# A Mamba block's output product on TensorE with plain and gamma-scaled weights, in place of GpSimd's gamma multiplication, in a new order of work

## The reference, cut to what matters

```python
h = tokens(x)                                             # 64 x 197 x 192
xz = layernorm(h) @ W_in;  x_inner, z = split(xz)         # 384 + 384
x_conv = silu(conv4(x_inner) + conv_b)
B, C = split(x_conv @ W_x);  delta = softplus(x_conv @ W_dt + b_dt)
s_t = exp(delta_t * A) * s_(t-1) + delta_t * x_t * B_t    # 384 x 16 states, 197 steps
y = (sum over states of s_t * C_t + D * x_conv) * silu(z)
out = y @ W_out
h = h + (out - mean) / sqrt(var + 1e-5) * gamma + beta    # the norm of this change
out = h + moe(layernorm(h))
```

## Time and profile before

| | |
|---|---|
| three runs | 2906.84, 2912.44 (median), 2925.01 us |
| the profiled execution | 2912.24 us, its span 2910.5 us |
| PE, DVE, ACT, POOL busy | 2502.9, 2273.4, 2123.5, 2312.8 us |
| mean granted PE clock | 0.927 of 2.4 GHz |

### The profile page before, as it was taken

The page is one execution under the profiler, slowest core; times in us unless marked ns, Lnnn a source line. Parts: engine busy times, 40 slices in busy tenths (PEclk is TensorE's granted clock), DMA queues, the critical chain, the costliest instruction groups (busy, mean ns, idle before and its releaser), DMA issues. The chain is left out here.

```text
span 2910.5 us, 37983 instructions
## 1 busy us (share of the span) xinstructions
PE 2502.9 (86%) x12595; PEld 1554.2 (53%) x12595; DVE 2273.4 (78%) x2290; ACT 2123.5 (73%) x4560; POOL 2312.8 (79%) x1158
## 2 busy tenths in 40 slices
PE   7788888888888889888888888888875478999997
PEld 4444444444445444444444444554431367888886
DVE  2799999999999999999999999999999664222222
ACT  3688888888888888988888888888885343334332
POOL 0589999999999999999999999999998242544442
PEclk9898999999999998999999999999985689999999
DMA  3555544555544455555445554445541034666652
GB/s 102 130 117 117 116 109 109 119 128 118 118 109 109 109 124 117 124 125 115 109 110 130 126 117 109 109 109 133 127 108 33 26 124 148 221 204 219 204 193 87
DMA packets 165466, 361.09 MB, mean 124 GB/s; under 512 B 18353, under 2 KB 89593, under 8 KB 157848
## 3 DMA queue, kind: packets, MB, share of 16 engines
q1 hardware_dynamic: 152504, 329.59, 45.0%
q0 software_dynamic: 12768, 29.08, 3.1%
HBM read 293.86 MB, written 69.30 MB: 125 GB/s over the span
## 5 line engine op out<-in xcount | busy, mean ns | idle before, releaser
L1532 DVE TENSOR_TENSOR_SCAN arena<-banks,arena 128x788 f32<-128x788 f32 x768 | 1350.2, 1788 | 120.9 <-ACT banks L731 91.0
L531 POOL TENSOR_TENSOR arena<-arena 128x1576 f32<-128x1576 f32 x384 | 1246.9, 3259 | 23.6 <-DVE arena L1532 23.5
L731 ACT ACTIVATE banks<-arena,neg_a 128x392 f32<-128x392 f32 x1536 | 833.5, 580 | 60.8 <-DVE arena L1532 58.4
L1521 DVE TENSOR_TENSOR arena<-arena,banks 128x1576 f32<-128x1576 f32 x320 | 568.1, 1775 | 19.8 <-PE banks L1099 16.7
L1115 PE MATMUL banks<-arena,gather_q 128*32 128x394 f32 x3072 | 373.9, 562 | 12.3 <-POOL arena L531 11.7
L1065 PE MATMUL banks<-arena,v_lo 128*128 128x394 f32 x768 | 307.2, 546 | 35.9 <-ACT arena L803 19.5
L689 POOL DMA_INDIRECT out_tokens<-arena x114 | 114.7, 1006 | 265.8 <-DVE arena L1731 246.6
L1044 PE MATMUL banks<-wtok,arena 128*99 128x192 f32 x1536 | 266.5, 331 | 57.7 <-ACT arena L881 31.1
L1716 DVE TENSOR_TENSOR arena<-banks,arena 128x384 f32<-128x384 f32 x57 | 31.8, 558 | 360.9 <-PE banks L1402 316.1
L1044 PEld LDWEIGHTS banks<-wtok,arena 128*99 128x99 f32 x1536 | 246.3, 167 | 101.2 <-ACT arena L881 51.0
L1012 ACT ACTIVATE arena<-banks 128x256 f32<-128x256 f32 x57 | 22.0, 385 | 326.3 <-PE banks L1368 305.3
(11 more groups left out here) (247 smaller groups left out, 4391.4 us busy)
## 6 DMA issues: line engine op xcount, KB each, us to landing
arena<-delta_du_scratch SPq DMA_DIRECT2D x384, 394.0 KB, 10.6
arena<-in_w_pack SPq DMA_DIRECT2D x57, 1155.0 KB
delta_du_scratch<-arena SPq DMA_DIRECT2D x96, 394.0 KB, 3.2
arena<-in_x SPq DMA_DIRECT2D x32, 1176.0 KB, 12.1
rows_scratch<-arena SPq DMA_DIRECT2D x32, 297.0 KB
rows_scratch<-arena SPq DMA_DIRECT2D x32, 294.0 KB
arena<-in_b SPq DMA_DIRECT2D x57, 96.0 KB
arena<-in_conv_w SPq DMA_DIRECT2D x1, 2304.0 KB, 11.3
```

What stands on the lines that cost most here:

```text
L531: pool.tensor_tensor(v[:, :, :], v[:, :, :], c_rep[r][:, u % NG].unsqueeze(1).to_broadcast([P, NQ, N2]), ALU.mult).then_inc(s_mulp, 1)
L731: ins = act.activation(o, d, ACT.Exp, scale=neg_a[:, c:c + 1])
L1521: dve.tensor_tensor(hb[(UNITS * n + u) % BUFS][:, :, :], rep[m][:, :, 1, :], ps_b[:, 0:N2].unsqueeze(1).to_broadcast([P, NQ, N2]), ALU.mul ...
L1532: dve.tensor_tensor_scan(v, decay[k % 2], v, 0.0, ALU.mult, ALU.add).then_inc(s_scan, 1)
```

## The change

1. A second weight set `wgam` = centred `wout` times gamma is made once at the start (gamma is now spread over 128 partitions). New PE products `out_gamma` b = 0, 1 multiply y by it into banks of their own.
2. `copy_out` is gone. `out_squares` reads the plain product from PSUM; the new `copy_gamma` copies the scaled one to `ob`; `out_norm` scales that. `apply_gamma` is gone, and `add_residual` waits for `out_norm`.
3. The three small deviation steps leave ACT: POOL does each before its power, with one `tensor_scalar`, or two `tensor_tensor` for the rows. For out and front this puts two instructions in POOL's order where there was one before the power's own wait.
4. A new order on PE, ACT, DVE and POOL. `silu_z` moves next to `silu_x` with one `exp_ln_tables` for both. `row_stats`, `rstd_rows` and `row_norm` move from body i+2 to body i+1 of their pair. SP's order is unchanged; its store of a pair's rows waits for `row_norm` as before.

The functions:

```diff
-        gam = sb("gam", [H0, DIM])
+        gam = sb("gam", [P, DIM])
+            def out_gamma(n, o, b):
+                if b == 0:
+                    pe.wait_ge(s_yev, MB * (n + 1))
+                    pe.wait_ge(s_wc, 2)
+                v = kbank(OG[b], o)
+                for f in range(2):
+                    c = b * L + f * HSTEP
+                    for k in range(MB):
+                        mm = pe.matmul(v[0:H0, f * DIM:(f + 1) * DIM], y[:, k, c:c + H0], wgam[:, k, :], start=(k == 0),
+                                       stop=(k == MB - 1))
+                mm.then_inc(s_ogmm, 1)
...
+            def out_squares(n, r, o, b):
                 act.wait_ge(s_opmm, 2 * n + b + 1)
...
+                for f in range(2):
+                    c = 2 * b + f
+                    ins = act.activation(rows[r][:, c, DIM:2 * DIM], kbank(OUT[b], o)[0:H0, f * DIM:(f + 1) * DIM], ACT.Square,
+                                         accum_out=sq2[:, c:c + 1])
+                ins.then_inc(s_oev, 1)
...
             def rstd_out(n):
                 need(pool, s_onorm, n)
+                pool.wait_ge(s_oev, 2 * (n + 1))
+                pool.tensor_scalar(var2[:, :], sq2[:, :], 1.0 / DIM, EPS, ALU.mult, ALU.add).then_inc(s_var2, 1)
                 pool.wait_ge(s_var2, n + 1)
...
+            dve.tensor_tensor(wgam[:, :, :], wout[:, :, :], gam[:, :].unsqueeze(1).to_broadcast([P, MB, DIM]), ALU.mult).then_inc(s_wc, 1)
```

PE's order, cut to the places of which the prediction speaks:

```diff
+                    if 1 in on and u == 0:
+                        pe.wait_ge(s_gev, 10 * (i + 1) + 2)
+                        dt(i + 1, o, r, DT + 2)
+                    if 1 in on and u == 0:
+                        pe.wait_ge(s_gev, 10 * (i + 1) + 3)
+                        dt(i + 1, o, r, DT + 1)
+                    if 1 in on and u == 0:
+                        pe.wait_ge(s_gev, 10 * (i + 1) + 4)
+                        dt(i + 1, o, r, DT)
...
+                    if -1 in on and u == 5:
+                        if 2 in on:
+                            pe.wait_ge(s_h, 2 * (i + 2) + 2)
...
+                        out_product(i - 1, r, 0)
...
+                    if -2 in on and u == 5:
+                        if i == PAIRS + 1:
+                            rank(FIRST, 1)
...
-            rank(FIRST, 1)
```

More of the change, by code:

```diff
@@ L514, in rstd_front @@
                 need(pool, s_hn, n)
+                pool.wait_ge(s_sq1, n + 1)
+                pool.tensor_scalar(var1[:, :], sq1[:, :], 1.0 / DIM, EPS, ALU.mult, ALU.add).then_inc(s_var[0], 1)
                 pool.wait_ge(s_var[0], n + 1)
@@ L521, in rstd_rows @@
                 need(pool, s_rows, n)
+                pool.wait_ge(s_mv3, n + 1)
+                pool.tensor_tensor(mv3[:, :, 0], mv3[:, :, 0], small[0:H0, 1, :], ALU.mult)
+                pool.tensor_tensor(mv3[:, :, 1], mv3[:, :, 1], small[0:H0, 2, :], ALU.add).then_inc(s_var[2], 1)
                 pool.wait_ge(s_var[2], n + 1)
@@ L554, in fill_rows, with add_residual @@
                                    ALU.add).then_inc(s_hbeta, 1)
-            def apply_gamma(n):
+            def add_residual(n, r):
                 pool.wait_ge(s_onorm, n + 1)
[L558 to L562, removed]
                 pool.wait_ge(s_hbeta, n + 1)
@@ L648, in body @@
                     if -1 in on and u == 9:
-                        rstd_out(i - 1)
+                        add_residual(i - 1, o)
+                    if -1 in on and u == 10:
+                        rstd_rows(i - 1)
                     if 0 in on and u > 0:
@@ L900, in body @@
-                    if -2 in on and k == 3:
-                        row_norm(i - 2, r)
+                        copy_product(i + 1, o, o, 1)
+                    if 1 in on and k == 1:
+                        silu_x(i + 1, o)
+                        exp_ln_tables()
+                    if 1 in on and k == 2:
+                        copy_product(i + 1, o, r, DT + 2)
                     if 0 in on and k == 3:
                         keep_b(i)
+                    if 1 in on and k == 3:
+                        copy_product(i + 1, o, r, DT + 1)
@@ new lines, in body @@
+                    if 1 in on and k == 5:
+                        softplus_up(i + 1)
+                    if 1 in on and k == 6:
+                        softplus_t(i + 1)
+                    if 1 in on and k == 7:
+                        softplus_ln(i + 1)
+                    if 1 in on and k == 8:
+                        middle_bc(i + 1, o)
+                    if 0 in on and k == 10:
+                        copy_c(i, r, r, 3)
+                    if 2 in on and k == 11:
+                        front_squares(i + 2, r)
@@ new lines, in body @@
+                    if 1 in on and k == 13:
+                        third_bc(i + 1, o)
+                    if 1 in on and k == 14:
+                        copy_product(i + 1, o, r, Z + 1)
+                    if -1 in on and k == 15:
+                        out_squares(i - 1, o, r, 1)
+                    if -1 in on and k == 16:
+                        copy_gamma(i - 1, r, 1)
+                    if -2 in on and k == 17:
+                        copy_back_t(i - 2, r, 1)
+                    if 2 in on and k == 17:
+                        front_norm(i + 2, r)
@@ L1612, in body @@
                         scan(i, k)
[L1613 to L1617 removed]
+                    if -1 in on and k == 5:
                         if i == PAIRS:
```

378 lines of the change are left out of this document (161 added, 217 removed).

## The result

The changed kernel takes 2927.68 us (2916.30 to 2935.11, 20 runs), the kernel before, in the same comparison, 2910.59 (2891.11 to 2928.18, 20 runs). The ratio is 1.0047, with a 95% interval of 1.0030 to 1.0064: slower by half a per cent, where I had forecast 0.6% faster. The profiled execution took 2930.19, its span is 2928.5, 18.0 more than that of before.

The account below looks back on a forecast made before the run. DVE and POOL, within 3 us of the period and joined by waits over ACT and PE, bound it. 64.5 + 1.8 + 0.1 + 0.7 = 67.1 us a pair against 67.45 (-10.5), ends -7.8: 2894 us, range 2862 to 2946.

Parts of the forecast that it names:

- within 1%: Whole kernel: a time that can't be told from no change, between 2883 and 2942 us; chance 0.42.
- DVE does the same work in another order: 64.5 a pair without waits.: DVE among the pairs: own work unchanged by the new order, 64.5 us a pair, to which new waits are added.
- a tensor_scalar of 4 columns isn't in the trace: POOL's new deviation step: no such instruction to price it by, between 0.20 and 1.02 us, taken as 0.20.
- Step A: Start of a pair: dt products wait for silu_x and delay spread_b(2) and bx(2); 1.5 to 2.2 us lost, taken as 1.8.
- my slow-dt rival: dt products at half rate behind PE's 2.1 us wait for silu_x: 68.7 us a pair, 2942 us; chance 0.27.
- Step B: From take_y0 to scan 18: PE waits under 1 us, scan 18 loses nothing, bx_pool9 0.1 us.
- step D: Back of a pair, behind decays 18: out_norm, add_residual, row_stats and row_norm all in time by tenths; cost 0.
- Step C: At out_product0: PE waits 3.0 us for embed1, the clock falls, decays 12 and 13 come late; 0.7 us lost.
- POOL, 64.5.: POOL's own need a pair: falls by 0.8 to 64.5 us without apply_gamma, tying with DVE's 64.5.
- The start, -2.: First pair: bc no longer ahead of dt on PE, 6 matmuls or 2 us before the first delta; -2 us.
- The end, -5.8.: Behind the last pair: DVE's 5.77 us wait for the first rank products goes as they move earlier; -5.8 us.

Follow-up runs that it names:

- The second form tried here: The changed kernel with front_stats' negated mean on DVE as a scalar_tensor_tensor with two SBUF inputs instead of a tensor_scalar; ratio 1.0024 to the kernel before.
- the kernel whose GpSimd was busy for 98.9% of the window: The kernel before, in its old order with gamma on POOL, with only front_stats' negated mean moved from DVE to ACT; 2849.54 us, ratio 0.9757.

## Why the prediction was wrong

The forecast was 2894, 0.6% faster; it is 0.5% slower. The measured time lies in the range of 2862 to 2946 and, by the 1% that I had named, in "within 1%"; the sign was wrong.

*"DVE does the same work in another order: 64.5 a pair without waits."* This is the step that failed. It was 65.07. It took every duration of before as the instruction's own. That of front_stats was set by where a POOL instruction happened to end, 0.55 to 1.07 us among the pairs, and the change moved that place, to 1.22 to 1.85. This is +0.70 a pair in the mean, 20 us, of a term that I had put at no change without a reason. I had also written that a tensor_scalar of 4 columns isn't in the trace. POOL had none, but front_stats on DVE is one, and its 0.56 beside the 0.20 that I took would have been the hint.

The Trainium skill (SBUF — State Buffer, SBUF: two separate sides) says that VectorE and GpSimd share a pair of ports, and that whichever starts first holds it for its whole instruction. The trace agrees in the main: 60 of 60 end with a POOL instruction. The section counts a VectorE operation in a two-port mode and, against a GpSimd operation that reads SBUF, one with two inputs in SBUF as users of the pair. The second form tried here has two such inputs, and it waits; whether the tensor_scalar ran in a two-port mode no run here shows. In two other runs one VectorE instruction of 30 was held not by the one POOL instruction that had started before it, but by three more that started behind it. The section would have warned of this step; I hadn't weighed it.

*Step A, 1.8 us (1.5 to 2.2).* It cost 0.82 + 1.33 + 0.28 = 2.43, which is +0.63 and nearly as much as the step above. The size was off because my forecast and my slow-dt rival are both true, in different pairs: dt takes 7.9 us in 19 of 30 and 6.2 in the others. The rival had 3.4 for the step (1.5 + 1.9); its pairs show 0.83 + 1.90 + 0.29 = 3.0. I had given it 0.27, and 19 of 30 pairs took its way.

*Step B, 0.1.* Right. PE waited 0.51 for take_y0 in the pair shown and 0.90 in the mean, kept its clock in all 29, and scan 18 has no gap. But the wait in front of scan 20, which was to go with it, stayed (0.29 before and 0.32 now in the mean); I count it under step D.

*Step C, 0.7.* Too high: 0.37 in the mean. out_product0 waited 1.20 for embed1, not 3.0, and ran at full rate (2.19 for 12). The clock fell later, behind a further 1.41, at z (the first two of L1075 took 1.68 in place of 0.82), and cost 1.08 at scan 14 in the ten of 29 periods in which dt had been fast.

*Step D, 0.* Nearly right: 0.32 at scan 20; the row norms themselves are in time, and the residual waits for out_norm 0.3 us at most.

*POOL, 64.5.* Right, if anything too high: the tensor_scalar took 0.20 to 0.21 as taken. But that it "ties" with DVE didn't hold once DVE's own need was 65.07: POOL idled 3.1 us a pair for scans. The offload was worth nothing in the time (the new order with gamma on POOL: 1.0040 against 1.0047), because the 1 us that it spares DVE at row_stats went into slow dt products.

*The start, -2.* It was +3.8. I had seen dt come earlier and not what bc then delays. The first bx, before, then after:

```profile
92.18 1.80 DVE L1521 TENSOR_TENSOR arena<-arena,banks 128x1576 f32<-128x1576 f32 x1 [16.75 <-PE banks L1099]
```

```profile
95.64 1.80 DVE L1530 TENSOR_TENSOR arena<-arena,banks 128x1576 f32<-128x1576 f32 x1 [17.82 <-PE banks L1084]
```

It waits for spread_b(0), which on PE stands behind the tokens' products. These now stand behind bc and start at 68.10 in place of 66.11. spread_b(0) itself now also stands behind a second conv product.

*The end, -5.8.* It was -8.4, and the 5.77 of the earlier trace rows are gone as said.

In sums: 67.1 became 67.1 + 0.57 (DVE's own time) + 0.63 (A) - 0.1 (B) - 0.33 (C) + 0.32 (D) = 68.2, as measured. That step C was too large by 0.33, and hides a part of the 1.2 us by which the first two terms were too small, is luck.

What stays open: why the same wait of 1.97 us leaves dt at full clock in some pairs and not in others. With gamma on POOL in the new order, 3 of 30 pairs were slow, behind waits of the same length. And why step D left 0.32 at scan 20 was not tried.

## What to carry to other kernels

A small instruction whose duration in the profile varies, here from 0.17 to 1.85 us, can hide a wait inside its busy time: compare its end with the ends on the other engines before you take its price, and treat that price as one that any new order can change. Relieving an engine pays only when it is what the others wait for, and a ratio of 1 can hide two effects that cancel. Here the same multiplication seemed worth nothing in one kernel and 1.7% in another, and in both the rows of who waited for whom showed about 1 us a pair that POOL's busy share didn't. Where a few tenths push TensorE's wait to where its clock falls, they are worth a multiple: here 0.64 us taken off DVE gave 2.1 us a pair, of which 0.5 (the run with three products more) to 1.0 (the waits at scans 18 and 20) are the clock's.

## What the runs showed of the hardware that I had not expected

A 99x4 arithmetic operation of VectorE with its operands in SBUF ended only when an instruction of GpSimd ended: 0.17 us with GpSimd idle, a median of 0.56 and 1.40 in the two orders, 1.37 as an instruction with two inputs. In the eight traces that have it among the pairs that holds for 240 of 240. In 238 it was the first instruction of GpSimd to end. In two, of 8.00 us each, it was the fourth, GpSimd's instructions having followed each other without a gap; one of them, in the changed kernel with the three added products:

```profile
261.77 8.00 DVE L1484 TENSOR_SCALAR arena<-arena 99x4 f32<-99x4 f32 x1
```

```profile
259.88 3.28 POOL L539 TENSOR_TENSOR arena<-arena 128x1576 f32<-128x1576 f32 x1
263.08 2.58 POOL L630 TENSOR_TENSOR arena<-arena 128x1182 f32<-128x1182 f32 x1
265.59 0.96 POOL L556 TENSOR_TENSOR arena<-arena 128x394 f32<-128x394 f32 x1
266.48 3.27 POOL L539 TENSOR_TENSOR arena<-arena 128x1576 f32<-128x1576 f32 x1
```

Not every operation of VectorE that stays in SBUF waits: the BATCH_NORM_STATS2 of row_stats took 0.33 to 0.35 us in all 112 instances among the pairs of the kernel before. The large scans and products of VectorE, which read one operand from PSUM, kept theirs: all 768 scans of the kernel whose GpSimd was busy for 98.9% of the window took 1.76 to 1.80 us.

Three products more on TensorE, which compute nothing that is kept, shortened a kernel by 0.7% in one place and 0.6% in another: they took the place of waits of 1.97 and 2.00 us. Behind 1.37 and 1.56 us the products kept their pace, and behind 2.31 they lost it in 30 of 30 pairs. Behind 1.97 they lost it in 19 of 30 pairs in one kernel and in 3 of 30 in another, so the length of the last wait alone doesn't decide.
